# Attention scores from keys per head, two heads side by side on the array, with two score buffers

## The chip, the cores and the metric

The kernel runs on one core of a Trainium2 chip. A core has TensorE (matmuls into PSUM, PE in the tables; PEld are its weight loads), VectorE (DVE), ScalarE (ACT), GpSimd (POOL), SyncE (SP, which issues DMAs) and 16 DMA engines. The engines run on their own and wait for each other by semaphores. The metric is the device time of one run in microseconds (us).

## The reference

Two layers, each an attention block over a latent context and a feed-forward block, on x of 8 x 100 x 1024 and a context of 8 x 722 x 256. Only the attention changes here. For layer 0 it is:

```
q_hk  = (layernorm(x) @ Wq.T).reshape(8, 100, 16, 128)
q_big = rope(einsum('bshk,hkq->bshq', q_hk, w_kc_q))          # 768 per head
kv_r  = rope(ctx)                                             # 722 x 256 per batch
q_r   = einsum('bshq,hqr->bhsr', q_big, W_qr)                 # 64 per head
k_r   = einsum('bld,hdr->bhlr', kv_r, W_kr)                   # 64 per head
attn  = softmax(einsum('bhsr,bhlr->bhsl', q_r, k_r), -1)
ctx_c = einsum('bhsl,bld->bhsd', attn, kv_r)
x     = x + (einsum('bhsd,hkd->bhsk', ctx_c, w_kc_kv) -> b,s,(h k)) @ Wo.T
```

Layer 1 is the same without rope on q. Layer 0's feed-forward is a mixture of 32 experts (4 per token), layer 1's a gated one with ternary weights. All of attention is float32.

## The kernel before

**Order.** Nothing plans the work: each engine's instructions stand in the order of its Python functions (`att_tensor`, `att_scalar`, `att_vector`, `att_pool`, `att_sync`), with semaphore waits written out by hand. An engine that waits holds up all that is queued behind it.

**Groups.** The 16 heads of a layer are worked in 4 groups of 4; groups 0 to 3 are layer 0, 4 to 7 layer 1. A group has a front, 8 batches, and an end.

**Front, layer 0.** For each head a and each of six pieces s, TensorE forms q_big (L745, two matmuls of 400 columns: 4 batches x 100 queries) beside a part of the next head's q_hk (L728). VectorE multiplies it by cosine and sine (L1210), GpSimd adds (L1320). `q_r` (L757) contracts the result to 64 coordinates in three visits per head, one half of the batches in each half of the array's columns. `q_c0` (L773) then goes back from 64 coordinates to the 256 of the latent space (q_c = q_r W_kr), one half of the batches in each half of the rows: 8 such pairs per group. ScalarE copies each result out of PSUM (L1029). In group 0 the context is roped and stored to kvT_d and kvN_d at the same time.

**Front, layer 1.** Without rope, the weights are folded (L787 to L813) so that q_r comes directly from x (`q_r1`, L823, two heads at once); `q_c1` (L837) is the counterpart of `q_c0`, again 8 pairs, two of them among the batches.

**Batches.** `scores` (L846) contracts the 256 latent coordinates: 6 chunks of 128 keys, each two matmuls of 400 columns (4 heads x 100 queries) into one of three PSUM banks. ScalarE evicts each chunk (L1114) into one of three buffers Sb. VectorE takes the maxima over the chunks (L1243), TensorE transposes them (`largest`, L923), VectorE reduces and negates (L1237), TensorE spreads the result (`spread`, L929), VectorE adds it (`shift`, L1231), ScalarE takes the exponential (L1105), VectorE sums (L1259), TensorE sums over partitions (`softmax_sum`, L866). `values` (L860) is 2 x 6 matmuls; VectorE scales them by the reciprocal (L1252, L1255). In step st TensorE does the scores of batch st, the largest and the spread of st-1, and the values and the sum of st-2. In layer 1 ScalarE also takes sums of |F| (L1061) of the last feed-forward's weights, three per batch.

**End.** `lift` (L943) and the output projection (L1002, L1005); before them the next group's first q_hk or folds.

**Loads.** SP loads kvT (two buffers) and kvN (three) per batch and the weights in one fixed order.

## Time and profile before

| | us |
|---|---|
| median of 3 runs | 3699.76 |
| lowest and highest run | 3695.35, 3700.8 |
| profiled execution: span, from first to last instruction | 3692.8 |
| TensorE busy | 3537.7 (96%) |
| VectorE busy | 1869.6 (51%) |
| ScalarE busy | 827.3 (22%) |
| GpSimd busy | 796.9 (22%) |
| attention of layer 0, about | 10 to 1290 |
| experts | 1290 to 2150 |
| attention of layer 1 | 2150 to 3145 |
| last feed-forward | 3145 to 3693 |

The page gives the profiled execution by its span; what lies before its first and behind its last instruction is not listed. A matmul's record runs until its results have landed, so that records of a stream overlap: the 400-column form has a mean of 501 ns, while such instructions follow each other every 336 ns. A float32 matmul is two instructions in the trace, a transpose one. "<-" names what ended a wait. Each instruction of a tile of 128 x 128 is written 128*128, then the moving operand's partitions x elements.

### The profile page before, as it was taken

The page shows a single profiled execution, that of the slowest core. Times are in us where ns is not written, and L with a number is a line of the kernel's source. Part 1 is how long each engine was busy: PE and PEld are TensorE (multiplying, and loading weights), DVE is VectorE, ACT ScalarE, POOL GpSimd, SP SyncE. Part 2 cuts the span into 40 slices and gives each one's busy share as a digit, 9 for nine tenths or more (in the row PEclk, how much of TensorE's full clock was granted, in tenths as well). Part 3 has the DMA queues.
Part 4 walks back from the last instruction along what each step waited for, and adds up shares of the span by engine and source line. Part 5 has one row for each costly group of instructions (what it writes and reads, how often), then busy time and mean ns, then how long its engine had stood idle before and what let it go on. Part 6 is the DMA issues. An engine that isn't in the chain of part 4 may idle for free.

```text
span 3692.8 us, 38083 instructions
## 1 busy us (share of the span) xinstructions
PE 3537.7 (96%) x14156; PEld 1746.1 (47%) x14157; DVE 1869.6 (51%) x1726; ACT 827.3 (22%) x1358; POOL 796.9 (22%) x745
## 2 busy tenths in 40 slices
PE   7899999999999969999999979999999999999999
PEld 4455455445445433333333345545455454554554
DVE  7785566468448551111111137638457286562561
ACT  1221032022022211111111125234143152220110
POOL 5600400220130012222222211000000011691660
PEclk9999999999999989999999989999999999999999
DMA  5621221122113176998888965335244151330320
GB/s 185 239 88 51 74 88 69 54 74 94 49 33 121 71 283 228 330 335 319 295 298 303 354 220 171 127 117 182 86 155 167 49 182 54 120 136 18 137 102 36
DMA packets 95088, 562.50 MB, mean 152 GB/s; under 512 B 11304, under 2 KB 13480, under 8 KB 77056
## 3 DMA queue, kind: packets, MB, share of 16 engines
q1 hardware_dynamic: 60784, 450.79, 32.2%
q0 software_dynamic: 30880, 93.75, 9.4%
q10 hardware_dynamic: 3312, 16.37, 1.2%
q8 instruction: 82, 1.34, 0.1%
q14 instruction: 30, 0.25, 0.0%
HBM read 523.13 MB, written 41.40 MB: 153 GB/s over the span
## 4 chain that ended last, share of the span: by engine, by line
PE 80%; DMA 7%; DVE 6%; issue 2%; ACT 2%; POOL 2%; SPq 1%; POOLq 0%; DVEq 0%; ACTq 0%
PE PS L860 12%; PE PS L846 12%; PE PS L1744 10%; PE PS L2062 9%; PE PS L1002 9%; DMA bias<-in_b 5%; PE PS L1768 5%; PE PS L2076 5%; PE PS L728 4%; PE PS L745 3%; PE PS L943 2%; PE PS L823 1%; PE PS L757 1%; PE PS L866 1%; POOL qrope L1320 1%
## 5 line engine op out<-in xcount | busy, mean ns | idle before, releaser
L846 PE MATMUL PS<-qc,kvT 128*128 128x400 f32 x1536 | 529.2, 501 | 14.9 <-DMA kvT<-kvT_d 5.6
L860 PE MATMUL PS<-Sb,kvN 128*128 128x400 f32 (+1 forms) x1536 | 539.3, 501 | 2.8 <-ACT Sb L1105 2.8
L1744 PE MATMUL PS<-W,hT 128*64 128x512 f32 x2208 | 504.4, 599 | 14.7 <-DMA bias<-in_b 10.8
L846 PEld LDWEIGHTS PS<-qc,kvT 128*128 128x128 f32 x1536 | 290.6, 190 | 242.7 <-ACT Sb L1114 8.8
L1320 POOL TENSOR_TENSOR qrope<-rt,rt 128x400 f32<-128x400 f32 x192 | 209.8, 1114 | 792.0 <-DVE rt L1210 792.0
L860 PEld LDWEIGHTS PS<-Sb,kvN 128*128 128x128 f32 (+1 forms) x1536 | 282.9, 190 | 197.4 <-ACT Sb L1105 4.8
L1837 DVE TENSOR_TENSOR gu<-PS,bias 128x512 f32<-128x512 f32 x69 | 47.7, 691 | 634.5 <-PE PS L1744 634.5
L2062 PE MATMUL PS<-xh,wq 128*128 128x400 f16 x2048 | 348.4, 334 | 1.5 <-DVE xh L1174 1.5
L2018 POOL TENSOR_SCALAR gtq<-stg,thr 128x1024 f16<-128x1024 f32 x96 | 294.9, 3086 | 192.9 <-DMA stg<-in_F 143.3
L1002 PE MATMUL PS<-wb,ctxl 128*128 128x512 f32 x768 | 331.7, 593 | 4.2 <-ACT ctxl L1029 4.2
L1243 DVE TENSOR_REDUCE mx<-Sb 128x400 f32<-128x2400 f32 x64 | 270.8, 4231 | 104.4 <-ACT Sb L1114 104.4
L1259 DVE TENSOR_REDUCE sums<-Sb 128x400 f32<-128x2400 f32 x64 | 272.4, 4257 | 87.1 <-ACT Sb L1105 87.1
L1744 PEld LDWEIGHTS PS<-W,hT 128*64 128x64 f32 x2208 | 153.2, 137 | 304.6 <-issue 286.9
L2062 PEld LDWEIGHTS PS<-xh,wq 128*128 128x128 f16 x2048 | 200.9, 98 | 148.9 <-issue 1.8
L1114 ACT ACTIVATE Sb<-PS 128x400 f32<-128x400 f32 x320 | 154.0, 503 | 454.2 <-PE PS L846 454.2
L1210 DVE TENSOR_TENSOR rt<-PS,ropeq 128x800 f32<-128x800 f32 x192 | 180.7, 983 | 146.0 <-PE PS L745 145.8
L1768 PE MATMUL PS<-W,actT 128*64 128x512 f32 x1104 | 250.3, 595 | 2.5 <-issue 2.5
L1002 PEld LDWEIGHTS PS<-wb,ctxl 128*128 128x128 f32 x768 | 145.3, 190 | 188.5 <-issue 179.9
L1276 DVE TENSOR_TENSOR X<-PS,X 128x512 f32<-128x512 f32 x96 | 66.3, 691 | 274.7 <-PE PS L1002 274.7
L1252 DVE RECIPROCAL rz<-PS 128x400 f32<-128x400 f32 x64 | 170.0, 2656 | 37.0 <-PE PS L866 37.0
L728 PE MATMUL PS<-xnT,wq_h 128*128 128x400 f32 x512 | 185.0, 499 | 0.5 <-ACT xnT L491 0.5
L1231 DVE TENSOR_TENSOR Sb<-Sb,PS 128x2400 f32<-128x2400 f32 x64 | 169.6, 2650 | 18.9 <-PE PS L929 18.9
(281 smaller groups left out, 3460.4 us busy)
## 6 DMA issues: line engine op xcount, KB each, us to landing
W<-in_W SPq DMA_DIRECT2D x96, 2048.0 KB, 10.1
kvT<-kvT_d SPq DMA_DIRECT2D x64, 768.0 KB, 5.7
kvN<-kvN_d SPq DMA_DIRECT2D x64, 768.0 KB, 4.3
stg<-in_F SPq DMA_DIRECT2D x32, 1536.0 KB, 6.5
absin<-in_F POOLq DMA_DIRECT2D x48, 512.0 KB, 3.9
hn<-in_F POOLq DMA_DIRECT2D x48, 512.0 KB, 3.9
wb<-in_WB SPq DMA_DIRECT2D x8, 2560.0 KB, 9.2
wc_h<-in_WC SPq DMA_DIRECT2D x32, 576.0 KB, 4.4
```

Source lines behind the costliest of these rows:

```text
L728: mm = nc.tensor.matmul(PS[:, half if a == 0 else 0, 0:HALF], wq_h[a % 2][:, c * K:(c + 1) * K], xnT[:, c, half * HALF:(half + 1) * HALF], ...
L846: mm = nc.tensor.matmul(PS[:, lc % 3, 0:GW], kvT[b % 2][:, dc, lc * P:(lc + 1) * P], qc[:, dc, b, :], start=dc == 0, stop=dc == CC - 1)
L860: mm = nc.tensor.matmul(PS[:, value_bank(b) + dc, 0:GW], kvN[b % 3][0:k, lc, dc * P:(dc + 1) * P], Sb[b % 3][0:k, lc, :], start=lc == 0, s ...
L1002: mm = nc.tensor.matmul(PS[:, 2 + n % 4, :], ctxl[:, a, m * P:(m + 1) * P], wb[:, w:w + 512], start=a == 0, stop=a == HA - 1)
L1243: nc.vector.tensor_reduce(mx[:, :], Sb[st % 3][:, :, :].rearrange("p c n -> p n c"), AX, ALU.max).then_inc(sem(f"{p}_mx"), 1)
L1259: nc.vector.tensor_reduce(sums[:, :], Sb[(st - 1) % 3][:, :, :].rearrange("p c n -> p n c"), AX, ALU.add).then_inc(sem(f"{p}_sum"), 1)
L1320: ins = nc.gpsimd.tensor_tensor(qrope[k % 4][:, i, :], rt[k % 2][0][:, i, :], rt[k % 2][1][:, 1 - i, :], ALU.add)
L1744: mm = nc.tensor.matmul(PS[g * BS:(g + 1) * BS, 2 + u % 2, :], hT2[k][:, c, half * BS:(half + 1) * BS], W2[:, q, o:o + N1], start=c == 0, ...
L1768: mm = nc.tensor.matmul(PS[h * BS:(h + 1) * BS, 4 + u % 2, :], actT[:, j, g * BS:(g + 1) * BS], W2[:, u % NQ_W, o:o + DH], start=c == 0, s ...
L2018: nc.gpsimd.tensor_scalar(gtq[q][:, w, :], stg[q][:, w, :], thr[:, w:w + 1], None, ALU.is_gt).then_inc(sem("f_gt"), 1)
L2062: mm = nc.tensor.matmul(PS[:, 4 * q + 2 * w + half, 0:HALF], wq[q][:, w, c, :], xh[part][:, c, half * HALF:(half + 1) * HALF], start=c == ...
L2076: mm = nc.tensor.matmul(PS[:, n % 8, :], hh[part][:, c, m * P:(m + 1) * P], wdq[:, c, half], start=c == 0 and part == 0, stop=c == EB - 1 ...
```

## The change

- **Keys per head.** q_c and its weights go. For each batch and each pair of heads u, `keys` forms k_r (64 coordinates of two heads in 128 partitions) by 2 x 2 matmuls of 363 columns from kvT and new weights wkr; ScalarE evicts each pair's 726 columns into KR (two buffers).
- **Scores** contract 64 coordinates: per chunk 4 matmuls, two heads each, the heads on the array's two row halves, with 121 keys stationary and 100 queries moving. Chunks are 121 keys (726 = 6 x 121) instead of 128. Two chunks share one pair of banks: chunks 0, 1, 4 and 5 banks 0 and 1; chunks 2 and 3 banks 2 and 3. The keys are written into the same four banks. ScalarE evicts 800 elements at a time, the last two chunks as 2 x 400.
- **Order of the batches.** The values of batch st-1, not st-2, are worked in step st, the keys of batch st+2 in two parts (early and late); Sb, KR and kvN have two buffers. ScalarE takes the exponential of batch st within step st, and the late keys' eviction behind it.
- **Maxima and sums** of VectorE are three tensor operations (800, 800, 400 elements) instead of a reduction of 2400.
- **q_r in bursts** of two pieces: 6 visits per group instead of 12, with six qrope buffers; the cosine product is written straight into qrope.
- In layer 1 the folds are put first in the front. SP's order of loads follows. The keys of batches 0 and 1 stand at the end of the front.

```diff
+LP = -(-L // LC)
...
+NR = 6
+NBST = 3 * HA // 2
+SCN, SEN = LC // 2, LC // 2 + 1
...
+                def next_kt(n):
+                    sp.wait_ge(sem(f"{p}_kr"), 2 * B * hg + 2 * (n - 1))
+                    kt(n % B)
+                def next_kn(n):
+                    sp.wait_ge(sem(f"{p}_cx"), 2 * B * hg + 2 * (n - 1))
+                    kn(n % B)
...
+            def q_r_burst(hg, j):
+                pe.wait_ge(sem(f"{p}_rope"), NQ * hg + 4 * j + 4)
+                for piece in (2 * j, 2 * j + 1):
+                    a, c = piece // 3, piece % 3
+                    if c == 0 and a >= 2:
+                        pe.wait_ge(sem(f"{p}_qre"), HA * hg + a - 1)
+                    for i in range(2):
+                        w = WC_R + (c + 3 * i) * R
+                        for half in range(2):
+                            at = (half + a) % 2 * R
+                            mm = nc.tensor.matmul(PS[at:at + R, 6 + a % 2, 0:HALF], wc_h[a % 2][:, w:w + R],
+                                                  qrope[(2 * piece + half) % NR][:, i, :],
+                                                  start=c == 0 and i == 0, stop=c == 2 and i == 1)
...
+        KEYS = [((2, 0), (2, 1)), ((3, 0), (3, 1)), ((4, 0), (4, 1)), ((5, 0), (5, 1)), ((6, 0), (6, 1)),
+                ((7, 0), None), ((7, 1), None), (None, None)]
+        KEYS_DONE = [3 + 2 * st for st in range(B - 1)] + [2 * B]
...
+            def keys(hg, b, u, st=None):
+                if u == 0:
+                    pe.wait_ge(sem(f"{p}_kt{b % 2}"), 16 * (4 * hg + b // 2 + 1))
+                if st is None:
+                    if b == 0 and u == 0:
+                        pe.wait_ge(sem(f"{p}_wr"), 16 * (hg + 1))
+                        if ly == 0:
+                            pe.wait_ge(sem(f"{p}_rt"), NQ * (hg + 1))
+                    elif b == 1:
+                        pe.wait_ge(sem(f"{p}_kre"), 2 * B * hg + u + 1)
+                else:
+                    pe.wait_ge(sem(f"{p}_se"), n_ev * hg + SEN * st + (2 if u else SEN))
+                w = b // BH * R if ly == 0 else 0
+                for dc in range(CC):
+                    for n in range(2):
+                        mm = nc.tensor.matmul(PS[:, 2 * u + n, 0:LH], wkr[:, dc, u, w:w + P], kvT[b % 2][:, dc, n * LH:(n + 1) * LH],
+                                              start=dc == 0, stop=dc == CC - 1)
+                mm.then_inc(sem(f"{p}_kr"), 1)
+            def scores(hg, b):
+                half, cols = b // BH, slice(b % BH * S, (b % BH + 1) * S)
+                for lc in range(LC):
+                    bank = 2 * (lc // 2 % 2)
+                    if lc == 0:
+                        if b == 0:
+                            if ly == 0:
+                                pe.wait_ge(sem(f"{p}_qre"), HA * (hg + 1))
+                            else:
+                                pe.wait_ge(sem(f"{p}_q1e"), 4 * (hg - g0) + 4)
+                        pe.wait_ge(sem(f"{p}_kre"), 2 * B * hg + KEYS_DONE[b])
+                        if b == B - 1:
+                            pe.wait_ge(sem(f"{p}_se"), n_ev * hg + SEN * b)
+                    elif lc == 2:
+                        if b < B - 2:
+                            pe.wait_ge(sem(f"{p}_kre"), 2 * B * hg + KEYS_DONE[b] + 1)
+                    elif lc == 4:
+                        pe.wait_ge(sem(f"{p}_se"), n_ev * hg + SEN * b + 1)
+                    for u in range(HA // 2):
+                        for r in range(2):
+                            rows, to = slice(r * R, (r + 1) * R), lc % 2 * 2 * S + u * S
+                            q = 2 * u + ((r + half) % 2 if ly == 0 else half)
+                            mm = nc.tensor.matmul(PS[0:LP, bank + r, to:to + S], KR[b % 2][rows, u, lc * LP:(lc + 1) * LP],
+                                                  QR[rows, q, cols], start=True, stop=True)
+                    if lc % 2:
+                        mm.then_inc(sem(f"{p}_sc"), 1)
...
+                scores(hg, 0)
+                keys(hg, 2, 0, 0)
+                largest(0)
+                keys(hg, 2, 1, 0)
+                spread(0)
+                for st in range(1, B - 1):
+                    early, late = KEYS[st]
+                    scores(hg, st)
                     if st >= 2:
-                        values(hg, st - 2, 0)
-                        softmax_sum(hg, st - 2)
-                    spread(st - 1)
-                    if st >= 2:
-                        values(hg, st - 2, 1)
+                        softmax_sum(hg, st - 1)
+                    keys(hg, *early, st)
+                    largest(st)
+                    values(hg, st - 1, 0)
+                    if st == 1:
+                        softmax_sum(hg, 0)
+                    spread(st)
+                    if late:
+                        keys(hg, *late, st)
+                    values(hg, st - 1, 1)
...
+                    for j in range(SCN):
+                        eng.wait_ge(sem(f"{p}_sc"), SCN * B * hg + SCN * st + j + 1)
+                        bank = 2 * (j % 2)
+                        to = Sb[st % 2][0:LP, 2 * j:2 * j + 2, :].rearrange("p l (r n) -> p l r n", r=2)
+                        src = PS[0:LP, bank:bank + 2, 0:GW].rearrange("p r (l n) -> p l r n", l=2)
+                        if j < SCN - 1:
+                            nc.scalar.activation(to, src, ACT.Copy).then_inc(sem(f"{p}_se"), 1)
+                        else:
+                            nc.scalar.activation(to[:, 0], src[:, 0], ACT.Copy).then_inc(sem(f"{p}_se"), 1)
+                            nc.scalar.activation(to[:, 1], src[:, 1], ACT.Identity, bias=cst[0:LP, C_PAD:C_PAD + 1]).then_inc(sem(f"{p}_se"), 1)
+                    early, late = KEYS[st]
+                    if early:
+                        c_key(hg, *early)
+                    elif not more:
+                        c_lift(0)
+                    elif ly == 1:
+                        fold(hg + 1, 0, 0)
+                    if ly == 1:
+                        for w in range(2):
+                            absolute(hg, 3 * st + w)
+                    if st == B - 1 and more and ly == 1:
+                        for n in range(1, 4):
+                            fold(hg + 1, 0, n)
+                    exponential(st)
+                    if late:
+                        c_key(hg, *late)
...
+                for st in range(B):
+                    maxima(st)
+                    negated(st)
+                    if st >= 1:
+                        inverse(st - 1)
+                    shift(st)
+                    column_sums(st)
+                    if st >= 1:
+                        scaled(st - 1)
+                inverse(B - 1)
+                scaled(B - 1)
```

The instruction order of TensorE in batch 1 of group 0, around the scores' third chunk. Before, the end of batch 1's scores, then largest and spread of batch 0, then batch 2's scores (kvT is the stationary latent context, mx and nmx the maxima; a_se is ScalarE's eviction):

```order
L846 MATMUL PS<-qc_94,kvT_178912_96 128x400 [waits a_se]
L846 MATMUL PS<-qc_94,kvT_178912_96 128x400
L846 MATMUL PS<-qc_94,kvT_178912_96 128x400 [waits a_se]
L846 MATMUL PS<-qc_94,kvT_178912_96 128x400
L923 MATMUL PS<-cst_50,mx_66 100x128 [waits a_mx]
L923 MATMUL PS<-cst_50,mx_66 100x128 x3
L929 MATMUL PS<-cst_50,nmx_69 128x100 [waits a_nm,a_qce]
L929 MATMUL PS<-cst_50,nmx_69 128x100 x3
L846 MATMUL PS<-qc_94,kvT_172768_95 128x400 [waits a_se,a_kt0]
L846 MATMUL PS<-qc_94,kvT_172768_95 128x400
L846 MATMUL PS<-qc_94,kvT_172768_95 128x400 [waits a_se]
L846 MATMUL PS<-qc_94,kvT_172768_95 128x400
```

After, from spread(0) on (KR and QR are the keys and queries of two heads, wkr the key weights; a_kre is ScalarE's eviction of keys):

```order
L982 MATMUL PS<-cst_50,nmx_70 121x100 [waits a_nm]
L982 MATMUL PS<-cst_50,nmx_70 121x100 x3
L894 MATMUL PS<-QR_73,KR_122272_74 121x100 [waits a_kre]
L894 MATMUL PS<-QR_73,KR_122272_74 121x100 x7
L894 MATMUL PS<-QR_73,KR_122272_74 121x100 [waits a_kre]
L894 MATMUL PS<-QR_73,KR_122272_74 121x100 x7
L894 MATMUL PS<-QR_73,KR_122272_74 121x100 [waits a_se]
L894 MATMUL PS<-QR_73,KR_122272_74 121x100 x7
L868 MATMUL PS<-kvT_185696_94,wkr_66 128x363 [waits a_se,a_kt1]
L868 MATMUL PS<-kvT_185696_94,wkr_66 128x363 x3
```

The largest and the spread of batch 0 stood behind the scores of batch 1 and now stand ahead of them; the third chunk waits for a key eviction.

TensorE in a later part of that batch: before, batch 2's largest, the values and the sum of batch 1, its spread:

```order
L923 MATMUL PS<-cst_50,mx_66 100x128 [waits a_mx]
L923 MATMUL PS<-cst_50,mx_66 100x128 x3
L860 MATMUL PS<-Sb_121568_73,kvN_191200_98 128x400 [waits a_cxe,a_kn1,a_ex]
L860 MATMUL PS<-Sb_121568_73,kvN_191200_98 128x400 x5
L866 MATMUL PS<-sums_67,cst_50 128x400 [waits a_sum]
L929 MATMUL PS<-cst_50,nmx_69 128x100 [waits a_nm]
L929 MATMUL PS<-cst_50,nmx_69 128x100 x3
L860 MATMUL PS<-Sb_121568_73,kvN_191200_98 128x400 x6
```

After, the corresponding part of batch 1, with the late keys (L868) between spread and second half of the values:

```order
L976 MATMUL PS<-cst_50,mx_99648_67 100x121 [waits a_mx]
L976 MATMUL PS<-cst_50,mx_99648_67 100x121 x3
L911 MATMUL PS<-Sb_133920_76,kvN_191520_95 128x400 [waits a_kn0,a_ex]
L911 MATMUL PS<-Sb_133920_76,kvN_191520_95 128x400 x5
L921 MATMUL PS<-sums_102848_68,cst_50 128x400 [waits a_sum]
L982 MATMUL PS<-cst_50,nmx_70 121x100 [waits a_nm]
L982 MATMUL PS<-cst_50,nmx_70 121x100 x3
L868 MATMUL PS<-kvT_185696_94,wkr_66 128x363 [waits a_se]
L868 MATMUL PS<-kvT_185696_94,wkr_66 128x363 x3
L911 MATMUL PS<-Sb_133920_76,kvN_191520_95 128x400 [waits a_rz]
L911 MATMUL PS<-Sb_133920_76,kvN_191520_95 128x400 x5
```

The values of a batch moved up by one step, and the sum's place with them.

ScalarE, batches 0 and 1 of group 0. Before (Sb are three buffers; L1105 is the exponential):

```order
L1114 ACTIVATE Sb_111968_72<-PS 128x400 [waits a_sc] x5
L1114 ACTIVATE Sb_111968_72<-PS,cst_50 128x400 [waits a_sc]
L1114 ACTIVATE Sb_121568_73<-PS 128x400 [waits a_sc] x5
L1114 ACTIVATE Sb_121568_73<-PS,cst_50 128x400 [waits a_sc]
L1114 ACTIVATE Sb_131168_74<-PS 128x400 [waits a_sc] x2
L1105 ACT_TABLE_LOAD
L1105 ACTIVATE Sb_111968_72<-Sb_111968_72 128x2400 [waits a_sb]
L1114 ACTIVATE Sb_131168_74<-PS 128x400 [waits a_sc] x3
L1114 ACTIVATE Sb_131168_74<-PS,cst_50 128x400 [waits a_sc]
```

After (L1088 evicts keys into KR, L1173 to L1176 scores, L1160 is the exponential):

```order
L1173 ACTIVATE Sb_133920_76<-PS 121x800 [waits a_sc] x2
L1175 ACTIVATE Sb_133920_76<-PS 121x400 [waits a_sc]
L1176 ACTIVATE Sb_133920_76<-PS,cst_50 121x400
L1088 ACTIVATE KR_128096_75<-PS 128x726 [waits a_kr]
L1160 ACT_TABLE_LOAD
L1160 ACTIVATE Sb_133920_76<-Sb_133920_76 121x2400 [waits a_sb]
L1088 ACTIVATE KR_128096_75<-PS 128x726 [waits a_kr]
L1173 ACTIVATE Sb_143520_77<-PS 121x800 [waits a_sc] x2
L1175 ACTIVATE Sb_143520_77<-PS 121x400 [waits a_sc]
L1176 ACTIVATE Sb_143520_77<-PS,cst_50 121x400
```

The exponential of batch 0 stood behind two whole batches of evictions; now it stands ahead of batch 2's late keys and of all of batch 1's scores.

## Rows read from the trace of the kernel before

**Rows 1.** The page: busy us (share, instructions); the chain that ended last, by line.
```profile
PE 3537.7 (96%) x14156; PEld 1746.1 (47%) x14157; DVE 1869.6 (51%) x1726; ACT 827.3 (22%) x1358; POOL 796.9 (22%) x745
...
PE PS L860 12%; PE PS L846 12%; PE PS L1744 10%; PE PS L2062 9%; PE PS L1002 9%; DMA bias<-in_b 5%; PE PS L1768 5%; PE PS L2076 5%; PE PS L728 4%; PE PS L745 3%; PE PS L943 2%; PE PS L823 1%; PE PS L757 1%; PE PS L866 1%; POOL qrope L1320 1%
```

**Rows 2.** The chain in order of time: start us, us, what.
```profile
528.90 8.06 PE PS L846 x24
...
546.51 8.06 PE PS L846 x24
...
779.50 16.39 PE PS L846 x48
```

**Rows 3.** Timeline, group 1, 528.5 to 547 us: start us, us, what.
```profile
537.24 4.20 PE L860 MATMUL PS<-Sb,kvN 128*128 128x400 f32 x12
...
541.95 0.51 PE L929 MATMUL PS<-cst,nmx 100*128 100x100 f32 x4
```

**Rows 4.** Timeline, the matmuls of L1784.
```profile
1347.81 0.52 PEld L1784 LDWEIGHTS PS<-gw,dup 128*128 128x128 f32 x4 [0.94 <-DVE gw L1517]
...
1347.81 0.68 PE L1784 MATMUL PS<-gw,dup 128*128 128x84 f32 x4 [0.77 <-DVE gw L1517]
```

**Rows 5.** Timeline, around L837's second but last visit in group 4.
```profile
2229.70 4.30 PE L846 MATMUL PS<-qc,kvT 128*128 128x400 f32 x12 [0.82 <-ACT Sb L1114]
...
2233.92 0.30 PEld L837 LDWEIGHTS PS<-qr,wk 64*128 64x128 f32 x4 [0.57 <-issue]
...
2233.92 0.94 PE L837 MATMUL PS<-qr,wk 64*128 64x400 f32 x4
```

**Rows 6.** Windows: stretch, us, busy us of PE, PEld, DVE, ACT, POOL; clock; DMA.
```profile
779.50:932.30 152.80, 151.92 (x497) 87.72 (x498) 119.98 (x47) 41.28 (x58) 0.00 (x0) 1.00 0.25 85
...
2458.30:2609.70 151.40, 148.23 (x513) 84.69 (x514) 117.91 (x46) 69.44 (x114) 12.69 (x24) 1.00 0.48 162
...
682.97:779.50 96.53, 92.75 (x324) 43.47 (x320) 46.54 (x51) 11.48 (x25) 48.41 (x48) 1.00 0.23 77
...
2423.20:2458.30 35.10, 32.06 (x133) 16.60 (x129) 4.75 (x9) 7.76 (x16) 0.00 (x0) 1.00 0.39 146
```

**Rows 7.** Timeline of the front of group 2.
```profile
716.45 0.94 PE L773 MATMUL PS<-qr,wc_h 64*128 64x400 f32 x4
...
717.32 1.61 PE L745 MATMUL PS<-qhk,wc_h 128*128 128x400 f32 x4
...
757.20 2.95 PE L745 MATMUL PS<-qhk,wc_h 128*128 128x400 f32 x8
...
768.67 1.89 DVE L1210 TENSOR_TENSOR rt<-PS,ropeq 128x800 f32<-128x800 f32 x2 [1.15 <-PE PS L745]
...
770.72 2.03 POOL L1320 TENSOR_TENSOR qrope<-rt,rt 128x400 f32<-128x400 f32 x2 [1.09 <-DVE rt L1210]
...
775.12 1.56 PE L757 MATMUL PS<-qrope,wc_h 128*64 128x400 f32 x8 [2.57 <-POOL qrope L1320]
...
777.33 1.61 PE L773 MATMUL PS<-qr,wc_h 64*128 64x400 f32 x8 [0.65 <-issue]
```

**Rows 8.** Groups by line and form: busy us, mean ns, idle before.
```profile
L1114 ACT ACTIVATE Sb<-PS 128x400 f32<-128x400 f32 x320 | 154.0, 503 | 454.2 <-PE PS L846 454.2
...
L491 ACT ACTIVATE xnT<-PS 128x1024 f32<-128x1024 f32 x12 | 11.8, 1017 | 10.5 <-PE PS L454 10.5
...
L1105 ACT ACTIVATE Sb<-Sb 128x2400 f32<-128x2400 f32 x64 | 140.7, 2199 | 111.9 <-DVE Sb L1231 111.9
...
L1231 DVE TENSOR_TENSOR Sb<-Sb,PS 128x2400 f32<-128x2400 f32 x64 | 169.6, 2650 | 18.9 <-PE PS L929 18.9
...
L1962 DVE TENSOR_TENSOR hh<-hid,hh 128x800 f32 x24 | 23.8, 992 | 0.0
```

**Rows 9.** Timeline and window, first scores of group 0.
```profile
166.39 17.90 PE L846 MATMUL PS<-qc,kvT 128*128 128x400 f32 x48 [4.39 <-DMA kvT<-kvT_d]
...
167.00:170.00 3.00, 3.00 (x6) 1.54 (x5) 0.00 (x0) 0.50 (x1) 0.00 (x0) 0.58 1.02 426
```

572 lines of the change are left out of this document (255 added, 317 removed).

## The prediction

> **What bounds the kernel now.** I read the page's busy shares first: TensorE is busy 96% of 3692.8 us. The page's chain of waits then says who sets the end: of its nine costliest entries eight are TensorE's lines, and the first two are the values (L860) and the scores (L846), 12% each [rows 1]. The chain in order of time shows how attention runs: batches follow each other every 17.61 us (528.90 to 546.51), 8.06 of it 24 score instructions [rows 2]. In the timeline of such a batch the values (12 instructions in two places) and the four small transposes of the spread follow without any idle time noted before them [rows 3]; VectorE's and ScalarE's work lies beside. So what the change does to TensorE's work counts in full, and so does each new wait of TensorE. The stages outside attention keep their code and order.
>
> There are 8 groups (4 heads each, 4 per layer) of 8 batches. I work group by group in the profiled execution. Its span is 3692.8 us; the median of the runs, 3699.8, is 7 us above it for what lies around the span, and I add the difference that I find to that median.
>
> **TensorE's work.** A 400-column matmul is two instructions of 336 ns (24 in 8.06 us [rows 2]). Scores before: 8 x 8.06 = 64.5 us per group. Keys now: per batch 16 instructions of 363 columns, 336 x 363/400 = 305 ns each, 4.88 us; 39.0 per group. Scores now: per batch 24 matmuls with 64 rows, 121 stationary and 100 moving columns, so 24 instructions in each half of the rows. No row shows that stream; two rows bound it. Weights of 128 columns under 84 moving columns follow each other every (0.52-0.19)/3 = 0.11 us [rows 4], so there the loads set the pace, and 121/128 of it is 0.106. The row-half pair of L837 puts four matmul instructions of 400 columns in 0.94 us [rows 5]; in turn they would need 4 x 0.334 = 1.34, so the halves run beside each other. Scores are then 24 x 0.106 = 2.54 us per batch; in turn they would be 5.09. I take 2.54, since L837 has the same shape of array.
>
> Going over to row halves costs too. The score instructions before L837 end their streaming at 2229.70+4.30-0.16 = 2233.83 (0.16 is the part of the last one's 0.50 us beyond its 0.34 of streaming); L837's first load starts at 2233.92, and 0.1 us passes until its weights are in [rows 5]. So 0.2 each way, 0.3 per batch on average, as a wait hides the leaving in many: 8 x 2.84 = 22.7 per group.
> The Trainium skill agrees (TensorEngine Tiling (Array Packing), Tiling Modes, Key Properties: a change of the tiling mode drains the array), and its section Performance Considerations, PSUM Bottleneck, speaks against the change: tiling makes the array faster, not the eviction of PSUM. The waits below are that rule in this kernel's terms; without it the sum would end at the next paragraph's gain.
>
> A group's scores thus go from 64.5 to 39.0+22.7 = 61.7, only 2.8 us less. More goes with q_c, 8 row-half pairs per group: one costs 716.45 to 717.32, 0.87, and 0.2 of uncovered loads on its two sides, 1.07; the last two of a layer-0 group with their waits 2.9 (776.63 to 779.50) [rows 7]. That is 6 x 1.07 + 2.9 = 9.3 per group, some 8 in layer 1. And q_r makes 6 visits instead of 12, each with about 0.3 of switching: 1.8 in layer 0. All: 8 x 2.8 + 4 x 9.3 + 4 x 8 + 4 x 1.8 = 99 us less work. Now where it goes.
>
> **Front of a layer-0 group** (groups 1 to 3; 96.5 us in group 2 [rows 6]). The last head's first q_big comes 757.20-682.97 = 74.2 us after the start [rows 6, 7]; four q_c and four q_r visits fewer put it at 68.7. The last head has no q_heads beside it: there the pace is VectorE's 1.9 us per piece and GpSimd's 2.0 [rows 7]. The products start at 70.5; burst 4 waits for GpSimd's piece 19 (76.2), which delays the last two pieces to 84.4. The first keys wait for these, since they write q_big's banks. Keys of batch 0 (4.9) end at 89.4, burst 5 (2.9) at 92.3, keys of batch 1 at 97.4. +0.9, with 9.8 us of keys in it that before were scores.
>
> **Front of a layer-1 group** (35.1 us in group 5 [rows 6]). Four q_c visits and their waits go. q_r1 21.5, folds 4.8, keys 9.8: 36.1, +0.9 (rounded).
>
> **The batches, layer 0** (152.8 us in group 2 [rows 6]). What stays: 152.8-64.5-0.9 (a wait before the first spread) = 87.4. With scores 22.7 and six batches of keys 29.3: 139.4. To this come waits. Prices: 0.2 us from the last streamed column to a reader; evictions of 400 elements 0.50 (0.46 in a row of several), of 1024 1.02, so 800 take 0.83 and 726 0.77; shift 2.65, exponential 2.2, a product of 800 elements 0.98 [rows 8].
> - Chunks 4 and 5 of the scores use the banks of 0 and 1: 0.2+0.83+0.04 = 1.07 after these, chunks 2 and 3 cover 0.85. 0.2, and 0.1 for weights not hidden: in 7 batches 2.1.
> - The early keys write banks 0 and 1, so they wait for the last two evictions, 0.2+0.46+0.58+0.04 = 1.3. Nothing covers it in batches 0 and 1 (1.4 each); the softmax sum and its switch (0.87) do in 2 to 5 (0.5 each): 4.8.
> - Batch 1: ScalarE takes its work in order, so the late keys of batch 2 are evicted only behind exponential(0), which needs shift(0): from the end of spread(0) 0.2+2.65+2.2+0.77+0.1 = 5.9 us. TensorE has only chunks 0 and 1 to do there (1.05) and waits 4.8. Before, with a third buffer, a whole batch of scores lay there. VectorE's order (reciprocal(0) ahead of shift(1)) adds 1.4 in batch 2.
> - Batches 6 and 7: without late keys TensorE has 7.1 us between the spread and the softmax sum, VectorE's shift, sums and scaling with the exponential need 8.6: 1.5 each, 3.0.
> Sum 16.1, less 0.6 where the last two overlap: 154.9, +2.1.
> **Layer 1** (151.4 [rows 6]): about 3 us of q_c pairs and waits that stood among the batches go, but ScalarE's sums of |F| put a wait of 1 us before chunk 4 four times: +0.8. The last group of each layer loses some 2.7 us of waits for the exponential: -0.4 and +0.2 instead.
>
> **Group 0.** SP's loads of kvT no longer queue behind the last q_r; they start 2 us sooner: -2 (between -5 and +2).
>
> Sum: -2 + 2 x (0.9+2.1) + (0.9-0.4) + 3 x (0.9+0.8) + (0.9+0.2) = +10.7 us.
>
> **The clock.** After a wait of 4.39 us 48 score instructions took 17.90 us, where group 2 has 16.39, and the granted clock is 0.58 in the window of 167 to 170 [rows 2, 9]: part of it ran at 1.2 and not 2.4 GHz. After 2.57 us of waiting L757 took its usual 1.56 [rows 7]. A wait of 4.8 us now stands in each group: 1.5 us each, +12 (0 to 3 each: 0 to 24).
> 10.7+12 = +23: **3723 us**.
>
> **Costed at nothing.** VectorE's three products for the maxima (0.98+0.98+0.57) end 3.0 us after the scores, the early keys at 3.8; a longer chain would add its rest to each batch. The key evictions, 1.54 us of ScalarE a batch, lie beside keys and values. kvT and kvN have two buffers, asked for in one line by SP; each is asked for over 10 us ahead of its use.
>
> **Rivals.**
> 1. Faster: loads of 64 rows may not set the pace, the 100 moving columns do. Four L929 take 0.51 us with 0.25 for the last: 0.087 each [rows 3]. 24 x 0.087 = 2.09 for 2.54, 64 times: -29; and with the clock held -12: **3682**. It decides where two chunks take under 0.75 us. Against it: L837's four loads take 0.30 us for two pairs, 0.11 apart, as with 128 rows [rows 4, 5]. 0.18.
> 2. No change: the waits are right, but the clock keeps its level and group 0 gains 5: **3706**. 0.16.
> 3. Much slower: the halves run in turn in so short a stream. +2.54 a batch, 163 us, less chunk 4's waits (17) and what batch 1's wait hides (7): **3862**. Against it L837's 0.94; but there only two pairs follow each other. 0.06.
> 4. Slower still than mine: in a half, load and matmul alternate, 0.106+0.087 = 0.193 an instruction, 4.6 us a batch: +2.1 x 64 = 134, less the same 24: **3833**. Against it: before, the loads lie wholly under the matmuls (24 instructions in 8.06 leave no room for them [rows 2]). 0.04. The Trainium skill has this as a rule (TensorE: Matmul & The Clock Gate, Part 3, What overlaps and what doesn't: a weight load overlaps running matmuls only in another row group); L846's rows disagree with it.
> 5. My forecast 0.56; its own range is 3700 to 3750.
>
> Range 3680 to 3775: down to rival 1, up to where the new waits are half again as long; 3 and 4 stay out. A measurement can tell 0.2%, 7.4 us, from none. Faster 0.19, same 0.17, slower 0.64.
>
> **What would show it.** Loads 0.106 apart in each half; one wait of 4.8 us per group on the key eviction at the third chunk of batch 1; waits on score evictions before chunk 4 and before the early keys in nearly every batch; 18.2 us from batch to batch where 17.61 stood; fronts of 97 and 36 us. I am wrong if a batch takes under 17.3 us, or over 20, or if batch 1 has no long wait.

## The result and the profile after

The changed kernel takes 3754.58 us (median of 4 runs, 3748.49 to 3757.65), the kernel before 3699.03 beside it (4 runs): 1.015 times, with an interval of 1.0136 to 1.0164. It is 55.6 us slower where I forecast 23 us slower. The direction was right and the time lies in the stated range, but the loss is 2.4 times the forecast, and where it arises was misjudged in two places: the front of group 0 and the clock behind the wait of batch 1.

The page of the profile after shows: busy us (share, instructions), the chain that ended last, by engine, and the groups of the new keys (L868) and scores (L894), each with its busy us, mean ns, and the idle time before it in us.

```profile
PE 3514.9 (94%) x16460; PEld 1831.4 (49%) x16461; DVE 1645.7 (44%) x1958; ACT 858.7 (23%) x1254; POOL 793.9 (21%) x745
...
PE 57%; issue 22%; DMA 7%; DVE 6%; POOL 4%; ACT 3%; SPq 1%; POOLq 0%; DVEq 0%; ACTq 0%
...
L868 PE MATMUL PS<-kvT,wkr 128*128 128x363 f32 x1024 | 358.0, 496 | 34.6 <-ACT Sb L1176 26.3
...
L894 PE MATMUL PS<-QR,KR 64*121 64x100 f32 x3072 | 209.1, 285 | 49.8 <-ACT KR L1088 37.0
```

Against [rows 1]: TensorE is busy 23 us less in a span 63 us longer. The two new groups name what now ends their waits: ScalarE, by its evictions of scores (Sb) and of keys (KR). A steady batch of group 1, from its first score to the next batch's:

```profile
545.32 3.12 PE L894 MATMUL PS<-QR,KR 64*121 64x100 f32 x48
548.37 0.94 PE L921 MATMUL PS<-sums,cst 121*128 121x400 f32 x2
549.62 2.69 PE L868 MATMUL PS<-kvT,wkr 128*128 128x363 f32 x8 [0.31 <-ACT Sb L1176]
552.15 0.58 PE L976 MATMUL PS<-cst,mx 121*100 121x121 f32 x4
552.56 4.20 PE L911 MATMUL PS<-Sb,kvN 121*128 121x400 f32 x12
```

The next batch's scores start at 563.61: 18.3 us a batch, where 18.2 were forecast and 17.61 stood before [rows 2]. The 8.06 us of scores are now 3.05 of scores and two times 2.6 of keys, and 0.31 us of waiting for the last score eviction. So the steady batch is as forecast; what was not foreseen lies elsewhere. Batch 1 of the same group:

```profile
499.80 1.09 PE L894 MATMUL PS<-QR,KR 64*121 64x100 f32 x16
505.51 3.58 PE L894 MATMUL PS<-QR,KR 64*121 64x100 f32 x32 [4.62 <-ACT KR L1088]
510.27 4.12 PE L868 MATMUL PS<-kvT,wkr 128*128 128x363 f32 x8 [1.18 <-ACT Sb L1176]
```

The wait is there (4.62, forecast 4.8). What follows it is slow: 32 scores in 3.58 us where other batches need some 2.0, eight key instructions in 4.12 instead of 2.69. The window says why (stretch, us, busy us of PE, PEld, DVE, ACT, POOL; granted clock; DMA share, GB/s):

```profile
502.96:513.20 10.24, 6.51 (x37) 5.18 (x38) 5.12 (x6) 5.05 (x6) 0.00 (x0) 0.50 0.00 1
```

The granted clock is at 0.50, the lower of its two levels (1.2 of 2.4 GHz), for 10.24 us. Such a stretch of 10.24 us follows the wait in six of the eight groups of this execution, one of 3.41 us in groups 0 and 2. ScalarE, seen in the same place:

```profile
502.59 2.20 ACT L1160 ACTIVATE Sb<-Sb 121x2400 f32<-121x2400 f32 x1 [5.19 <-DVE Sb L1306]
504.70 0.76 ACT L1088 ACTIVATE KR<-PS 128x726 f32<-128x726 f32 x1
```

The eviction on which TensorE waits stands behind an exponential that itself waits for VectorE's shift. The eviction itself takes 0.76 us and its keys were ready; only the written order holds it back, as experiment 1 shows.

By stages, from two profiled executions of each kernel (the first and a second one made for this purpose), in us:

| stage | before | after |
|---|---|---|
| group 0, first query head to first scores | 137.6, 137.6 | 147.8, 148.4 |
| fronts of groups 1, 2, 3 | 98.4 97.1 97.1, 97.1 97.1 97.1 | 99.9 98.2 99.8, 99.9 99.9 99.8 |
| first scores to lift, group 0 | 156.5, 155.6 | 159.0, 160.6 |
| the same, groups 1 and 2 | 152.8 152.8, 152.8 152.8 | 158.8 158.9, 160.2 159.0 |
| group 3, scores to end | 198.8, 198.8 | 204.5, 204.0 |
| between layers, with group 4's front | 934.1, 938.4 | 944.2, 937.9 |
| fronts of groups 5 to 7 | 35.4 to 35.8 | 36.5 |
| scores to lift, groups 4, 5, 6 | 151.9 151.4 151.3, 151.9 151.4 153.1 | 156.2 153.9 156.2, 156.0 153.8 156.1 |
| group 7, scores to end | 201.9, 201.9 | 203.8, 203.7 |

(The groups' ends, 54.2 us, are the same everywhere. The fronts are counted here from 0.6 us before the point from which [rows 6] counts, so 97.1 is the 96.5 of [rows 6].) Apart from group 4's front, the stage between the layers has the same code in both kernels; it scatters by 4 us in one kernel and 6 in the other. The other rows repeat within 2 us. Added up over the eight groups, the stretches from the scores on (to the lift, in groups 3 and 7 to the end) take 1317 and 1318 us before, 1351 and 1353 after; below this sum is called the batches' total.

### The profile page after: what moved, and what is told of

Read it like the earlier page. It is cut to its first block, busy times and chain, and to the rows that moved or that the text cites. A ratio compares the mean times of both kernels' runs of the same rounds, so it can differ in the third digit from the quotient of the medians.

```text
span 3756.0 us, 42823 instructions
## 1 busy us (share of the span) xinstructions
PE 3514.9 (94%) x16460; PEld 1831.4 (49%) x16461; DVE 1645.7 (44%) x1958; ACT 858.7 (23%) x1254; POOL 793.9 (21%) x745
## 4 chain that ended last, share of the span: by engine, by line
PE 57%; issue 22%; DMA 7%; DVE 6%; POOL 4%; ACT 3%; SPq 1%; POOLq 0%; DVEq 0%; ACTq 0%
PE PS L1825 10%; PE PS L2144 9%; PE PS L911 7%; PE PS L1061 6%; PE PS L868 6%; DMA bias<-in_b 5%; PE PS L1849 5%; PE PS L2158 4%; POOL qrope L1398 4%; PE PS L848 2%; PE PS L894 2%; DVE Sb L1306 1%; PE PS L998 1%; ACT Sb L1160 1%; DMA kvT_d<-cT 1%
## 5 line engine op out<-in xcount | busy, mean ns | idle before, releaser
L911 PE MATMUL PS<-Sb,kvN 121*128 121x400 f32 (+1 forms) x1536 | 537.7, 500 | 0.0
L868 PE MATMUL PS<-kvT,wkr 128*128 128x363 f32 x1024 | 358.0, 496 | 34.6 <-ACT Sb L1176 26.3
L911 PEld LDWEIGHTS PS<-Sb,kvN 121*128 121x128 f32 (+1 forms) x1536 | 285.2, 190 | 204.7 <-DVE rz L1322 3.6
L1398 POOL TENSOR_TENSOR qrope<-qrope,rt 128x400 f32<-128x400 f32 x192 | 209.3, 1112 | 793.8 <-DVE rt L1275 793.6
L2100 POOL TENSOR_SCALAR gtq<-stg,thr 128x1024 f16<-128x1024 f32 x96 | 291.7, 3053 | 180.9 <-DMA stg<-in_F 131.9
L868 PEld LDWEIGHTS PS<-kvT,wkr 128*128 128x128 f32 x1024 | 197.3, 201 | 170.4 <-issue 81.9
L2144 PEld LDWEIGHTS PS<-xh,wq 128*128 128x128 f16 x2048 | 201.1, 98 | 148.9 <-issue 2.6
L894 PE MATMUL PS<-QR,KR 64*121 64x100 f32 x3072 | 209.1, 285 | 49.8 <-ACT KR L1088 37.0
L1061 PEld LDWEIGHTS PS<-wb,ctxl 128*128 128x128 f32 x768 | 145.3, 190 | 188.5 <-issue 179.9
L894 PEld LDWEIGHTS PS<-QR,KR 64*121 64x121 f32 x3072 | 186.1, 193 | 93.8 <-ACT KR L1088 40.4
L1160 ACT ACTIVATE Sb<-Sb 121x2400 f32<-121x2400 f32 x64 | 141.0, 2203 | 384.3 <-DVE Sb L1306 384.0
L1306 DVE TENSOR_TENSOR Sb<-Sb,PS 121x2400 f32<-121x2400 f32 x64 | 169.4, 2647 | 76.4 <-PE PS L982 76.4
L1291 DVE TENSOR_TENSOR mx<-Sb 121x800 f32<-121x800 f32 x64 | 63.2, 988 | 252.3 <-ACT Sb L1173 252.3
```

The lines of the kernel that those rows point to most:

```text
L868: mm = nc.tensor.matmul(PS[:, 2 * u + n, 0:LH], wkr[:, dc, u, w:w + P], kvT[b % 2][:, dc, n * LH:(n + 1) * LH], start=dc == 0, stop=dc == ...
L894: mm = nc.tensor.matmul(PS[0:LP, bank + r, to:to + S], KR[b % 2][rows, u, lc * LP:(lc + 1) * LP], QR[rows, q, cols], start=True, stop=True)
L911: mm = nc.tensor.matmul(PS[:, value_bank(b) + dc, 0:GW], kvN[b % 2][0:k, lc, dc * P:(dc + 1) * P], Sb[b % 2][0:k, lc, :], start=lc == 0, s ...
L1061: mm = nc.tensor.matmul(PS[:, 2 + n % 4, :], ctxl[:, a, m * P:(m + 1) * P], wb[:, w:w + 512], start=a == 0, stop=a == HA - 1)
L1160: nc.scalar.activation(Sb[b % 2][0:LP, :, :], Sb[b % 2][0:LP, :, :], ACT.Exp).then_inc(sem(f"{p}_ex"), 1)
L1306: nc.vector.tensor_tensor(sb, sb, PS[0:LP, 5, 0:GW].unsqueeze(1).to_broadcast([LP, LC, GW]), ALU.add).then_inc(sem(f"{p}_sb"), 1)
```

## The experiments

The time is the median of the runs given. The kernel before ran beside each (medians 3697 to 3700 us), and 3755 stands for the changed kernel. Experiments 7, 8 and 13 are single profiled runs, read by their stages. Experiment 7 leaves out half of some keys' contraction, and 8 contracts both heads of a pair over the rows of the first, so neither computes the reference's values. The code is shortened to the lines that matter, in part put in words.

**1. The order at a group's start.** ScalarE and VectorE take batch 1's scores before the exponential and the sums of batch 0.

```
 ScalarE, step 0:
-  c_key(2,0); exponential(0); c_key(2,1)      step 1: evictions of scores(1) ...
+  c_key(2,0); c_key(2,1); evictions of scores(1); exponential(0)
 VectorE, step 0:
   maxima(0); negated(0); shift(0)
+  maxima(1)
   column_sums(0)
```

> The changed kernel, with another order on two engines at each group's start: ScalarE evicts the late keys of batch 2 and batch 1's scores before exponential(0), VectorE takes batch 1's maxima before the column sums of batch 0. Theory (a long wait in batch 1, and the clock that falls behind it): the 4.6 us wait before batch 1's third chunk goes (8 x 4.6 = 37), and with it the 10.24 us at half clock that stand behind it in six of eight groups (keys at 4.12 in place of 2.6 us, 32 scores in 3.58: some 4.5 us a group, 27): 3755 - 64 = 3691 us. Rival 1 (the slow stretches have another cause and stay): 3755 - 37 = 3718. Rival 2 (the wait only moves on, to the exponential or the sums that now come later): 3745 to 3755.

Measured: 3690.21 us (3684.9 to 3700.09, 10 runs), 0.9986 of before, interval 0.9974 to 0.9997. The kernel before had 3697.1 beside it. The theory said 3691. Of the same place in its timeline:

```profile
493.78 3.12 PE L894 MATMUL PS<-QR,KR 64*121 64x100 f32 x48
498.08 2.69 PE L868 MATMUL PS<-kvT,wkr 128*128 128x363 f32 x8 [1.18 <-ACT Sb L1176]
```

48 scores in a row and keys at their usual 2.69: the wait and the slow stretch behind it are both gone. Only a stretch of 3.41 us at the lower clock is left among the late batches of five groups. Groups 1 and 2 now take 152.9 us from scores to lift, and the batches' total is 1291 us, 60 to 62 less than in the changed kernel. The order of a few items at each group's start cost 64 us by the medians, more than the whole of the loss.

**2 to 4. The wait kept, but filled.** Matmuls whose result nobody reads stand under batch 1's wait, so only the clock is changed.

```
 elif lc == 2:
+    if b == 1:
+        for _ in range(FILL):      # 11, 6, 3
+            nc.tensor.matmul(PS[:, 6, 0:HALF], ones, QR[:, 0, :], start=True, stop=True)
```

> The changed kernel, with 11 further matmuls of 400 columns (3.7 us of TensorE, into a bank that is free then, the result unused) in each group between chunks 1 and 2 of batch 1's scores, where TensorE waits 4.6 us. They stand under the wait, so they cost nothing by themselves and take no wait away. Theory (the wait pulls the clock down, which is a term of its own of 4 to 5 us a group): the 10.24 us at half clock behind it go, 6 x 4.5 = 27 us faster, 3728. Rival 1 (the clock costs the 1.5 us a group of the prediction): 3755 - 12 = 3743. Rival 2 (the clock falls for another reason): 3755 as before, or slower by what of the filling is not hidden (up to 0.5 us a group, 4).

Measured with 11: 3751.07 us (3747.61 to 3753.45, 4 runs). The expectation misjudged the filling: it took a 400-column matmul for 0.334 us, but that is one of its two instructions. In the trace:

```profile
498.67 7.66 PE L889 MATMUL PS<-QR,cst 128*128 128x400 f32 x22
```

So 22 instructions took 7.4 us and stood some 2.8 beyond the wait. That the time did not rise by those 8 x 2.8 = 22 us suggested that the clock was worth over 20 us; the next run was made to fit.

> The changed kernel, with 6 further matmuls of 400 columns (result unused) in each group under the 4.6 us wait of batch 1. A 400-column matmul is two instructions of 336 ns, so these take 4.0 us and end before the wait does; the 11 of the run with the longer filling took 7.4 us and stood 2.8 us beyond it, 22 us in eight groups, beside a time that fell by 3.5. Theory (what stands behind the wait at half clock costs some 25 us in all): no stretch at half clock behind batch 1's wait, 3755 - 26 = 3729. Rival (the clock costs the prediction's 12, and the filling before gained elsewhere): 3743. Rival 2 (the clock costs nothing): 3755.

Measured with 6: 3733.51 us (3725.86 to 3738.01, 4 runs), 21 below the changed kernel; 3729 was expected.

```profile
498.19 4.30 PE L889 MATMUL PS<-QR,cst 128*128 128x400 f32 x12
502.89 1.94 PE L898 MATMUL PS<-QR,KR 64*121 64x100 f32 x32 [0.40 <-ACT KR L1092]
506.00 2.69 PE L869 MATMUL PS<-kvT,wkr 128*128 128x363 f32 x8 [1.18 <-ACT Sb L1180]
```

```profile
502.50:513.00 10.50, 8.93 (x57) 6.05 (x58) 5.48 (x7) 3.66 (x6) 0.00 (x0) 1.00 0.00 0
```

The 32 scores take 1.94 instead of 3.58 us, the keys 2.69 instead of 4.12, the clock is at 1.00. TensorE still can't go on sooner than before, so what is gained is the clock's term by itself: 21 us by the medians, whose runs scatter by 12. By the stages it is 25 to 27: the batches' total is 1326 us, where the changed kernel has 1351 and 1353. The profiled run took the median's time, but 149.8 us of it in group 0's front, which this edit doesn't touch and which takes 147.8 and 148.4 in the changed kernel. That is part of the difference.

> The changed kernel, with 3 further matmuls of 400 columns (2.0 us) under batch 1's wait instead of 6: some 2.6 us of it stay empty. With 4.6 empty the median is 3755, with 0.4 empty 3733.5. Theory (the clock's cost is no share of the wait but comes whole or in part with a stretch of 3.41 us at half clock; a wait of 2.6 us before the keys of the front is followed by one such stretch): one stretch of 3.41 us behind the wait in most groups, 1.7 us each: 3733 + 14 = 3747. Rival 1 (a wait of 2.6 us costs nothing in clock): 3733. Rival 2 (it costs as much as one of 4.6): 3755.

Measured with 3: 3750.87 us (3739.88 to 3756.1, 4 runs), between the theory's 3747 and rival 2's 3755, which the scatter doesn't tell apart; rival 1 (3733) is refuted.

```profile
503.16 2.55 PE L898 MATMUL PS<-QR,KR 64*121 64x100 f32 x32 [2.41 <-ACT KR L1092]
506.88 4.79 PE L869 MATMUL PS<-kvT,wkr 128*128 128x363 f32 x8 [1.17 <-ACT Sb L1180]
```

```profile
504.20:511.00 6.80, 5.63 (x25) 3.78 (x22) 3.43 (x5) 1.82 (x3) 0.00 (x0) 0.51 0.00 0
```

With 2.41 us empty, and 1.17 after it, there are 6.8 us at the lower clock behind the wait in five groups, where the theory had 3.4. Group 0 has 3.4 there, groups 4 and 6 none. The batches' total is 1346 us, 5 to 7 less than unfilled and 20 more than with 6. Half of the wait filled buys little, all of it 25 to 27 us: the clock's cost is no fixed share of the wait.

**5. Rows of 6144 bytes, 121 partitions kept.**

```
-kvT_d = nc.dram_tensor("kvT_d", [B, P, CC * LPAD], ...)
+kvT_d = nc.dram_tensor("kvT_d", [B, P, CC * LC * P], ...)      # cT and kvT in SBUF likewise
```

> The changed kernel, with kvT kept in rows of 6144 bytes instead of 5808, in DRAM and in SBUF (42 columns per half more that nobody reads); the 121 keys per chunk stay. Theory (the shorter rows are what halves the rate of the context's stores): kvT_d's stores land in 4.7 us again instead of 8.3, ScalarE's waits for them in group 0's front go from 45 to some 12 us, the clock keeps its level there, and the front of group 0 falls from 147.8 to 138: 10 us faster, 3745. Rival (the store of 121 partitions ahead in the same queue is the cause): no change in the median, 3755, with stores at 8 us.

Measured: 3754.81 us (3750.48 to 3757.66, 5 runs). The theory falls: the stores land in 8.6 us, and the front of group 0 takes 147.9 us, not 138.

**6. 128 partitions, rows of 5808 bytes kept.**

```
-kvN_d = nc.dram_tensor("kvN_d", [B, LP, LC * DC], ...)
+kvN_d = nc.dram_tensor("kvN_d", [B, P, LC * DC], ...)
-eng.dma_start(kvN_d[b], crope[b % 2][0:LP, :, :]...)
+eng.dma_start(kvN_d[b], crope[b % 2][:, :, :]...)              # the load likewise
```

> The changed kernel, with kvN stored and loaded over 128 partitions instead of 121 (7 rows that nobody reads); kvT's rows stay at 5808 bytes. Theory (the short rows of kvT halve the stores' rate): no change, 3755. Rival (the 121 partitions are the cause): kvT_d's stores land in under 5.5 us, the front of group 0 falls by up to 10 us, 3745.

Measured: 3751.32 us (3746.14 to 3756.64, 4 runs). In the median that can't be told from 3755, but the rival's mechanism is plain. The DMA issues of 30 to 175 us (KB each, median us to landing), of the changed kernel, of rows of 6144 bytes, and of 128 partitions:

```profile
kvT_d<-cT ACTq DMA_DIRECT2D x8, 726.0 KB, 8.3
```
```profile
kvT_d<-cT ACTq DMA_DIRECT2D x8, 768.0 KB, 8.6
```
```profile
kvN_d<-crope ACTq DMA_DIRECT2D x8, 768.0 KB, 4.0
kvT_d<-cT ACTq DMA_DIRECT2D x8, 726.0 KB, 5.5
```

The store of kvT_d is slow because the store of kvN_d in front of it in the same queue has 121 partitions: in all eleven profiles with 121 partitions kvT_d lands in 7.8 to 8.6 us, in the three with 128 in 5.5 to 6.1. It is no matter of bytes: both stores moved more of them before, in 3.3 and 4.7 us. ScalarE's waits for kvT_d, which must have left the one buffer cT, by the waits in 30 to 175 us (us in total, times, longest), before, after, and with 128 partitions:

```profile
ACT cT L578 <- DMA kvT_d<-cT: 10.5, 5, 3.8
```
```profile
ACT cT L582 <- DMA kvT_d<-cT: 45.2, 7, 8.2
```
```profile
ACT cT L586 <- DMA kvT_d<-cT: 16.2, 5, 4.6
```

The front of group 0 takes 145.4 us here. That can't be set against 147.8 as it stands, since this front scatters with the time that it spends at the lower clock: in eight profiles with the changed kernel's code there (the changed kernel's two and those of experiments 1 to 4, 8 and 10) it takes 145.3 to 150.5 us, 148.0 on average, with 10 to 24 us at the lower clock. The three with 128 partitions (6, 11 and 12) take 145.4, 143.4 and 142.5. So the stores cost some 4 us of the front, which no median here can show. The Trainium skill has the rule that I should have weighed (DMA: Bandwidth & Descriptors, "Why a DMA increments its semaphore by 16 and not by 1", How many engines): a transfer uses the largest number of engines up to 16 that divides the outermost dimension of both its sides. By that rule 121 partitions would give 11 engines and 128 give 16, an estimate from that section. No view here names the engines or says when the store of 121 partitions itself lands; the order of the landing times behind it fits the rule and doesn't prove it.

**7. Half the keys' work in group 0's front.** Where the rest of the front's loss is.

```
-for dc in range(CC):
+for dc in range(1 if st is None and hg == 0 else CC):
```

> The changed kernel, with half of the keys' work left out in the front of group 0 alone (batches 0 and 1 contract one half of the coordinates: 16 instructions instead of 32, each half taking 4.9 us at full clock). Theory (the prediction's term for group 0's front, -2, left out that its keys now stand between the last context transposes and the first scores, where no keys stood before; TensorE is the only one late there): the first scores come 4.9 to 5.2 us sooner after the first instruction of the query heads (147.8 us now, 142.7 then). Rival (the front waits for the kvT load anyway, as before, and the keys hide under it): 147.8 again, with a wait for kvT's load ahead of the keys.

Measured: the first scores come 143.1 us after the first query head. Without the edit it is 145.3 to 150.5, so this difference alone would be weak. The chain behind the last context transpose (L573 and its like) is steadier: it takes 11.4 us here and 14.8 to 16.2 in the eight profiles without the edit. There is no wait for kvT:

```profile
161.65 5.60 PE L796 MATMUL PS<-qrope,wc_h 128*64 128x400 f32 x16 [0.66 <-ACT cT L582]
167.18 5.26 PE L869 MATMUL PS<-kvT,wkr 128*128 128x363 f32 x16
172.37 3.12 PE L895 MATMUL PS<-QR,KR 64*121 64x100 f32 x48
```

Against the changed kernel itself:

```profile
160.60 1.04 PE L573 MATMUL PS<-cst,crope 121*128 121x121 f32 x4 [0.76 <-ACT cT L582]
162.30 4.24 PE L796 MATMUL PS<-qrope,wc_h 128*64 128x400 f32 x16 [0.66 <-ACT cT L582]
166.47 10.05 PE L868 MATMUL PS<-kvT,wkr 128*128 128x363 f32 x32
176.45 1.81 PE L894 MATMUL PS<-QR,KR 64*121 64x100 f32 x28
```

And before, where a wait for kvT's load led to the scores ([rows 9]):

```profile
158.88 0.81 PE L569 MATMUL PS<-cst,crope 128*128 128x128 f32 x4
160.38 1.61 PE L773 MATMUL PS<-qr,wc_h 64*128 64x400 f32 x8 [0.69 <-ACT cT L578]
```

The keys are on the path in full. From the end of the last transpose to the first scores the kernel before takes 6.7 us, 4.39 of it that wait, and the changed one 14.8: the last burst of q_r (4.24, part of it at the lower clock), then 10 us of keys. The whole kernel took 3755.13 us in this one run, from which the 5 us can't be read.

**8. Both heads on one half of the rows.**

```
-rows = slice(r * R, (r + 1) * R)
+rows = slice(0, R)
```

> The changed kernel, with the scores of both heads of a pair on rows 0 to 63 (the second head's scores are then those of other rows), so 48 instructions follow each other in one half instead of 24 in each. It measures what two halves give. Theory (the halves run beside each other, and in each the loads set the pace): 48 x 0.106 = 5.1 us a batch instead of the 3.12 seen, +2.0 x 64 = 127 less what waits before chunk 4 and of batch 1 are hidden (20): 3862. Rival 1 (the pace is that of the moving columns, 0.087, or half of the seen 0.065 comes from one port that both share): 3.1 us a batch again, 3755. Rival 2 (with a single half, load and matmul alternate: 0.19 each): 9.3 us a batch, over 4100.

Measured: 3902.01 us in one run. A batch of group 1:

```profile
574.24 5.32 PE L894 MATMUL PS<-QR,KR 64*121 64x100 f32 x48
```

5.32 us for 48, 0.11 each, against 3.12 in two halves: the halves do run beside each other, and within a half load and matmul don't alternate, which would take 9.3. By the Trainium skill's rule (TensorE: Matmul & The Clock Gate, Part 3, cited in the prediction) no load could overlap a matmul here, since all rows are the same; the 5.32 us disagree with it. The total is 147 above, where the expectation had 127 less 20 that waits would hide, 107. Nothing was hidden: the batches' total is 1490 us, 137 to 139 more, some 8 x 8 x 2.2. Of the rest 7 to 13 us lie in the stage between the layers (951.4 here).

**9. q_r after each piece.** The part "q_r in bursts" undone.

```
-NBST = 3 * HA // 2        # 6 visits of 16 instructions a group
+NBST = 3 * HA             # 12 visits of 8
-for piece in (2 * j, 2 * j + 1):
+for piece in (j,):
```

> The changed kernel, with q_r's matmuls issued after each piece (12 visits of 8 instructions a group) instead of in bursts of two pieces (6 visits of 16). Theory (a visit costs 0.3 us of switching on TensorE, and the front of a layer-0 group is TensorE's but for its last head): 6 visits x 0.3 x 4 groups less what lies in the last head's waits: 3760, +5 (+2 to +7). Rival 1 (the burst has a price of its own: the last pieces wait for burst 4 and the last burst is twice as long, so single visits end the front sooner): 3745. Rival 2: no difference, 3755.

Measured: 3743.09 us (3741.6 to 3749.15, 4 runs): rival 1, in the median. The stages say how much of it is real: the fronts of groups 1 to 3 take 97.0, 96.9 and 96.8 us, some 3 less each, and the stage between the layers, which this edit doesn't touch, happened to take 935.8. The end of group 1's front, with bursts (of a second execution of the changed kernel) and with single visits:

```profile
469.11 2.91 PE L796 MATMUL PS<-qrope,wc_h 128*64 128x400 f32 x16 [0.61 <-POOL qrope L1398]
471.95 2.95 PE L781 MATMUL PS<-qhk,wc_h 128*128 128x400 f32 x8
477.52 6.82 PE L868 MATMUL PS<-kvT,wkr 128*128 128x363 f32 x16 [2.61 <-DVE rt L1275]
```
```profile
471.00 2.95 PE L781 MATMUL PS<-qhk,wc_h 128*128 128x400 f32 x8
473.88 1.56 PE L796 MATMUL PS<-qrope,wc_h 128*64 128x400 f32 x8
476.56 5.13 PE L868 MATMUL PS<-kvT,wkr 128*128 128x363 f32 x16 [1.12 <-DVE rt L1275]
```

The burst waits for GpSimd's later piece and holds q_big's last pieces back behind it, TensorE then waits 2.61 us for their products, and the clock falls: the keys take 6.82 us instead of 5.13. The clock's part can be told apart, since in one front of the changed kernel's six it kept its level: that front (group 2, first profile) takes 98.2 us. So of the 3 us the burst itself costs 1.3 and the clock behind it 1.7. The switching that a burst saves is worth less.

**10. The sum in the spread's bank** (on top of 1).

```
 def z_bank(b):
-    return 4 if b == B - 1 else 7
+    return 4 if b == B - 1 else 5 if b else 7
 softmax_sum: no wait for scaled(b - 1); spread(b >= 2) waits for reciprocal(b - 1)
```

> The kernel with the other order at each group's start (3690 us), and of the three further edits only the softmax sum of batches 1 to 6 in the spread's bank. The three together gave 3651. Theory (each wait counts by itself): 3.0 of the 4.1 us a group go, 24: 3666; the key banks then hold some 15 of the rest. Rival (the sum's wait only becomes a longer one of the early keys behind it, since both stand behind the same stretch of ScalarE): under 10 us of gain, 3682.

Measured: 3671.67 us (3670.43 to 3678.69, 4 runs), 18.5 less than 3690.21, where the theory had 24 and the rival under 10: the theory's side, some of it given back.

**11. Three edits together** (on top of 1): the sum's bank; 128 partitions as in 6; and the key units' banks.

```
-keys(b, u) write banks 2 * u and 2 * u + 1
+early units write banks 2 and 3, late ones 0 and 1 (b >= 2)
```

> The kernel with the other order at each group's start (3690 us), with three further edits: kvN over 128 partitions (group 0's front 2 us shorter); the softmax sum of batches 1 to 6 in the spread's bank, so that it no longer waits for the scaling of the batch before (1.05 + 1.52 + 1.53 us a group seen); early key units in banks 2 and 3, which are evicted first, late ones in 0 and 1 (waits of 1.18 twice and 0.31 three to four times a group seen, of which 0.5 comes back before batch 1's scores). Theory (these waits of TensorE are on the path, each for itself): sums 3.0 of the 4.1, keys 2.8 of the 3.3, together 5.8 x 8 = 46, and 2: 3642 us. Rival 1 (VectorE is the next bound: maxima, reciprocal and spread take the place of half of it): 3665. Rival 2 (nothing gained, since VectorE's chain of the batch sets the pace): 3690.

Measured: 3650.62 us (3645.85 to 3658.38, 4 runs), 0.9871 of before (0.9849 to 0.9892). Groups 1 and 2 take 146.8 us from scores to lift. It is 9 us above the theory's 3642: of the sum's waits 1.1 us in two pieces stay in group 1; 0.46 us came back before batch 1's scores, as expected, and 1.11 before batch 2's, which was not. The batches' total is 1253 us, against 1272 in experiment 10 and 1291 in experiment 1: 19 us for the keys' banks (22 expected) and as much for the sum's.

**12. All edits, with single visits.**

```
 11, with experiment 9's edit
```

> The kernel with all four edits of order and banks (3651 us), and q_r's matmuls issued after each piece. With single visits alone the fronts of groups 1 to 3 took 96.9 us instead of 99.9, since the last pieces wait less for burst 4 (2.61 us before the keys became 1.12) and the 3.41 us at half clock behind that wait go. Theory (that is the burst's own price, and it adds to the other edits): 3 x 3 = 9 less, 3642. Rival (what single visits gained in the median, 11.5, was the scatter of the stage between the layers alone): 3651.

Measured: 3639.94 us (3637.63 to 3640.41, 4 runs), 0.9837 of before (0.9821 to 0.9854). 10.7 us less than 11, where the theory had 9; but only half of it is the theory's doing. The fronts take 96.9, 97.0 and 96.8, where 11 had 98.2, 98.2 and 99.8, since there the clock fell in one of the three alone: 5.5 us less. The rest is scatter of other stages. This version beats both kernels, the changed one by 115 us and the one before by 59. The granted clock's mean in it is 0.987, in the changed kernel 0.972.

**13, 14. Both kernels once more.**

> The kernel before once more, for the stages whose code did not change. Between the last group of layer 0 and the first scores of layer 1 the profile before has 934.1 us, the one after 944.1, of which 1.4 are the front of layer 1's first group. Theory (this stage scatters from execution to execution by some 8 us, as it does over seven kernels with the same code there, 935.8 to 942.8): the stage takes 934 to 941, and the attention of both layers agrees with the first profile within 3 us. Rival (the changed kernel makes it slower): 934 again within 1 us.

Measured: 3699.07 us; the stage between the layers 938.4, attention within 2.2 us of the first profile in layer 0 and 1.6 in layer 1. That is what the theory said.

> The changed kernel once more, timed on the chip and with the runs of before that the other kernels of this call have. Theory: 3755 within 4, its attention stages as in the first profile within 3 us, and the stage between the layers anywhere from 936 to 945. Rival (what differs between the layers belongs to the kernel): 944 again, and the kernel with single visits for q_r (3743, its stage 935.8) is faster by its own doing.

Measured: 3755.68 us (3752.06 to 3758.84, 4 runs), 1.0146 of before; the stage 937.9, layer 1's attention 942.0 (942.3), layer 0's 1294.5 (1289.6, a group more with a long slow stretch, which is over the 3 us expected). So the 10 us that stood between the first two profiles in this stage were scatter for the most part.

## Why the forecast was too small, step by step

Right:
- **Stream of the scores.** 0.106 us per load in each half: 48 in one half take 5.32 (0.11). Scores with their switch and chunk 4's wait were to take 3.1; 3.05 from the first to the sum.
- **The batches' waits.** Batch 1: 4.62 for 4.8. Early keys: 1.18 in batches 0 and 1 for 1.4, 0.31 in three later ones for 0.5 in four. The sum: 1.05 and twice 1.53 for 1.4 and twice 1.5. The waits before chunk 4 were named for nearly every batch; the profile shows twelve, all in layer 1 (9.2 us in all). The clock kept up by filling, groups 1 and 2 take 155.7 us from scores to lift: +2.9 against [rows 6], with 2.1 forecast. Layer 1: 151.2 in groups 5 and 6, for 151.4 before; +0.8 forecast.
- **PSUM evictions, in part.** The Trainium skill's PSUM Bottleneck (TensorEngine Tiling (Array Packing), Performance Considerations), cited in the prediction, fits the small waits of the early keys, which end at ScalarE's evictions. It doesn't explain the long one: that eviction takes 0.76 us, TensorE's 4.62 lasted for the exponential ahead of it, and experiment 1 removes the wait with the same evictions.
- **Layer 1's front.** 35.9, counted as in [rows 6], for 36.1.
- Rivals 1, 3 and 4 are refuted by the batch of 18.3 us and by experiment 8; rival 2 by the clock, which did not keep its level, and by group 0, which lost 10 us instead of gaining 5.

Failed:
- **"Group 0 ... -2".** It was +10.2 and +10.8, a mistake of 12 us in one place. The step corrected one item of the old chain, the start of kvT's loads. But behind the last context transpose the chain is another: the wait for the load is gone, and 10 us of keys and a q_r burst partly at the lower clock stand there, 14.8 and 15.9 us for 6.7 and 5.7 before. Even by the forecast's own numbers, 9.8 us of keys behind a load that ends 2 sooner, the term was +7.8. Ahead of that point the 121-partition stores, which I had not weighed at all, cost some 4 us: with 128 partitions the last transpose ends 127.4 to 129.5 us after the first query head, with 121 it ends at 130.3 to 134.3, before at 130.9 and 131.9.
- **"A wait of 4.8 us now stands in each group: 1.5 us each, +12".** The wait, its place and the fall of the clock were right; the size was not. It was read from one wait of 4.39 us [rows 9], behind which the lower clock lasted 3.4 us, and here it lasts 10.24 us in six of eight groups. Filled, the term is 21 us by the medians and 25 to 27 by the stages, at or beyond the end of the stated 0 to 24: +13 to +15 by the stages.
- **"Front of a layer-0 group ... +0.9".** Counted as in [rows 6], the one front of six in which the clock kept its level takes 97.6 us for the forecast 97.4, so that its chain, burst 4 and the wait for the products, was right. The other five take 99.2 or 99.3: behind the wait the clock falls (keys at 6.82 us), which the sum had at nothing: it went by the wait of 2.57 us of [rows 7], behind which L757 took its usual time. With three groups some 4 us.
- **Last groups, -0.4 and +0.2.** With the wait filled group 3 takes 201.2 us from scores to end, 2.4 above before, and group 7 201.1, 0.8 below: 2 us in all beside the forecast.
- **A term left out.** The sum has no batches for group 0, +2.1 by its own working. It cost nothing: filled, they take 155.7 us, where they took 156.5 and 155.6 before, with the slow scores of [rows 9] in them.

The forecast's 23 with 12 (group 0), 14 (clock), 4 (fronts) and 2 (last groups) makes 55, for the measured 55.6. The first three were found by experiments; that the sum meets the median to 1 us is luck, since group 0's front and the stage between the layers scatter by some 5 us each. The 7 us that the prediction puts "around the span" are also misread: in every run on record the time is 1.7 us above the span, so most of the 7 us are the profiled execution against the median. As only a difference was added to that median, it did no harm. "Costed at nothing" held: VectorE's maxima, the key evictions and the buffers of kvT and kvN ended no wait of note, but the order of these evictions did, as said.

So the change as a whole is not slow by its arithmetic. TensorE's work fell, and what it lost came from the order at the groups' starts (64 us with its clock), from the sum's bank, the keys' banks, the stores of 121 partitions and the bursts. Whether the kernel before would gain from edits of the same kind was not tried, so 3640 against 3699 is not the worth of the change alone.

## What to carry to other kernels

When a buffer or bank is taken away, look at each in-order engine for an item that stands behind one with a long wait of its own, and move it ahead: here that was worth more than the arithmetic that the change was about. Price a wait of TensorE like those seen here, 2.4 to 4.6 us, by what follows at the lower clock as well, which a shorter wait did not reduce in proportion. And where a stage starts differently from the others (a first group), rebuild its whole chain instead of correcting the one item that changed.

## What the runs showed of the hardware that was not expected

- A wait of 4.62 us was followed by 10.24 us at 0.50 in six of eight groups, one of 2.41 us (and 1.17) by 6.80 us at 0.51 in five of eight. Behind one of 0.40 us it was none, but for 3.4 us in group 4, where waits of 0.67 and 1.18 came next. In time: 3755, 3751 and 3733.5 us.
- Behind a store of 121 partitions, which has fewer bytes than one of 128, the next store in the same queue took 8.3 us to land, behind one of 128 partitions 5.5 (7.8 to 8.6 and 5.5 to 6.1 over all profiles).
- In one half of the rows 48 loads of 64 x 121 with their matmuls of 100 columns took 5.32 us, in two halves 3.12.
- A stage with the same code (about 938 us, rich in DMA) took between 934 and 944 us in the profiles, and 951 in experiment 8, whose values differ. A difference of ten microseconds between two kernels is to be looked for by stage before it is explained.
